# Pair 0's beginning: three small pieces of work put elsewhere in the queues

## What is computed

```python
def _dequant(qweight, scales, qzeros, g_idx):
    w = (qw[:, None, :] >> shifts[None, :, None] & 15).reshape(-1, N)
    z = ((qz[:, :, None] >> shifts[None, None, :] & 15) + 1).reshape(G, -1)
    return (w - z[g_idx]) * scales[g_idx]
...
Wg, Wu, Wd = _dequant(gate ...), _dequant(up ...), _dequant(down ...)
h = silu(xf @ Wg) * (xf @ Wu)
out = h @ Wd
...
x = x + 0.5 * ffn(layernorm(x))
x = x + attn(layernorm(x))
x = x + 0.5 * ffn(layernorm(x))
```

## Time and profile before

| | |
|---|---|
| three runs | 834.16, 834.57, 834.84 us |
| median | 834.57 us |
| the profiled execution: its time | 834.31 us |
| its span, first to last instruction | 832.5 us |
| TensorE busy | 816.9 us, 98% |
| TensorE idle in the first 30 us | 10.5 us |

### The profile page before, as it was taken

How to read it: one execution, slowest core, us unless ns; L and a number is a source line. 1 busy time by engine, 2 the same in 40 slices (tenths; PEclk the granted TensorE clock), 3 DMA queues, 4 the chain that set the end, 5 groups by cost and what they waited for, 6 DMA issues and landing times.

```text
span 832.5 us, 10583 instructions
## 1 busy us (share of the span) xinstructions
PE 816.9 (98%) x3944; PEld 671.9 (81%) x3944; DVE 493.2 (59%) x809; ACT 272.8 (33%) x471; POOL 251.2 (30%) x203
## 2 busy tenths in 40 slices
PE   5999999999999999999999999999999999999998
PEld 4777778878888888788888888888878888888786
DVE  7899945766554544547766785546346644443452
ACT  3333433455111111333656871121123311211221
POOL 5555614752115061303064371062411200110100
PEclk9999999999999999999999999999999999999999
DMA  5998968865754532334053159544444155444131
GB/s 157 268 347 276 311 202 286 335 254 222 277 189 140 170 133 70 105 107 152 1 178 126 39 178 373 207 139 166 126 154 154 43 197 170 133 150 153 29 102 51
DMA packets 73405, 143.04 MB, mean 172 GB/s; under 512 B 26092, under 2 KB 37028, under 8 KB 68362
## 3 DMA queue, kind: packets, MB, share of 16 engines
q1 hardware_dynamic: 66964, 131.10, 46.4%
q10 hardware_dynamic: 5526, 7.04, 2.4%
q0 software_dynamic: 864, 4.23, 1.8%
HBM read 104.30 MB, written 37.98 MB: 171 GB/s over the span
## 4 chain that ended last, share of the span: by engine, by line
PE 94%; DVE 2%; DMA 1%; POOL 1%; issue 1%; SPq 1%; ACT 1%; DVEq 0%; POOLq 0%
PE ps L811 52%; PE ps L804 38%; PE ps L822 2%; PE ps L1198 2%; DMA qs<-in_L_ffn_up_qweight 1%; DVE xn L1741 1%; SPq L561 1%; POOL wp L2213 0%; DMA zq_gu<-in_L_ffn_up_qzeros 0%; DVE stats L1718 0%; PE ps L890 0%; PE ps L1123 0%; POOL wd L2213 0%; DVE pT L1707 0%; ACT pr L1562 0%
## 5 line engine op out<-in xcount | busy, mean ns | idle before, releaser
L804 PE MATMUL ps<-blk,ring 128*128 128x512 f32 (+1 forms) x1386 | 321.2, 390 | 0.6 <-DVE u L1710 0.5
L804 PEld LDWEIGHTS ps<-blk,ring 128*128 128x128 f32 (+1 forms) x1386 | 256.5, 185 | 59.2 <-issue 1.2
L811 PE MATMUL ps<-wd,hT 128*128 128x512 f32 (+1 forms) x1056 | 251.7, 391 | 0.2
L811 PEld LDWEIGHTS ps<-wd,hT 128*128 128x128 f32 (+1 forms) x1056 | 196.9, 188 | 42.7 <-DVE h L1877 0.5
L2265 POOL TENSOR_TENSOR h<-h,u 128x512 f32<-128x512 f32 (+1 forms) x33 | 42.7, 1293 | 322.9 <-ACT h L1446 322.9
L811 PE MATMUL ps<-xT,wp 128*128 128x512 f32 x480 | 112.8, 391 | 0.2 <-POOL wp L2213 0.2
L811 PEld LDWEIGHTS ps<-xT,wp 128*128 128x128 f32 x480 | 89.8, 188 | 19.9 <-issue 0.6
L1710 DVE TENSOR_TENSOR u<-ps,p1s 128x512 f32<-128x512 f32 (+1 forms) x66 | 45.4, 687 | 97.0 <-PE ps L804 97.0
L1446 ACT ACTIVATE h<-h 128x512 f32<-128x512 f32 (+1 forms) x33 | 20.9, 632 | 177.7 <-DVE h L1710 177.7
L1710 DVE TENSOR_TENSOR h<-ps,p1s 128x512 f32<-128x512 f32 (+1 forms) x33 | 22.8, 691 | 64.3 <-PE ps L804 64.3
L1710 DVE TENSOR_TENSOR u<-ps,u 128x512 f32<-128x512 f32 (+1 forms) x66 | 45.6, 691 | 25.3 <-PE ps L804 24.3
(11 more groups left out here) (130 smaller groups left out, 887.2 us busy)
## 6 DMA issues: line engine op xcount, KB each, us to landing
ring<-wsaved SPq DMA_DIRECT2D x29, 1024.0 KB, 5.1
ring<-wsaved SPq DMA_DIRECT2D x33, 768.0 KB, 4.3
wsaved<-wp SPq DMA_DIRECT2D x10, 1024.0 KB, 5.2
stream<-xres SPq DMA_DIRECT2D x32, 256.0 KB, 2.3
xn<-stream SPq DMA_DIRECT2D x8, 1024.0 KB, 6.8
xres<-stream SPq DMA_DIRECT2D x32, 256.0 KB, 3.5
wfull<-wf ACTq DMA_DIRECT2D x20, 256.0 KB
wsaved<-wp SPq DMA_DIRECT2D x10, 512.0 KB, 4.9
```

Of the source, the lines that this page charges most:

```text
L804: mm = pe.matmul(ps[0:w, bank, :], ring[:, slot, which, a, kt, 0:w], blk[:, which, b, kt, :], start=not onto and kt == 0 and n == 0, stop= ...
L811: mm = pe.matmul(bank_ap, lhs(a), rhs(b), start=first and n == 0, stop=last and n == 2)
```

## The change

- DVE: the unpacking of down's zeros stands behind `tab_first` and the unpacking of unit 0, and no longer ahead of the one-hot steps. The step that makes `tab_first` is now number PACK + 3 of `s_tab`.
- SP: the loads of units 1 and 2 stand ahead of the transfers of down's indices and zeros. The transfer of down's scales to `rows_d` moves from SP to POOL's queue, near its start.
- POOL: the four index steps, and the wait for the table `rows_d`, stand behind the low half of unit 0.
- ACT: of the six transfers to `tab_rest` the first part's two stay where they were; the other four stand behind the high half of unit 2.
- PE: `keep_warm(5)` for `keep_warm(8)`, two tiles of x are turned ahead of `scales_zeros(0)`, and the `keep_warm(1)` there is gone.

```diff
-        ZERO_STEPS, ZERO_D_STEPS, TAB_STEPS = PACK + 2, 2 * PACK + 3, 2 * PACK + 4
+        ZERO_STEPS, TAB_STEPS, ZERO_D_STEPS = PACK + 2, PACK + 3, 2 * PACK + 4
...
-            return d_sz[i % 2], 16 * (i // 2 + 1)
+            return d_sz[i % 2], 16 * (i // 2 + 1 + (i + 1) % 2)
...
# SP
+            load_units(sp, [1])
 
             sp.wait_ge(s_cst, 4)
...
-            sp.dma_start(rows_d[:, 0:HID], scales[2]).then_inc(d_rows, 16)
-            load_units(sp, [1])
+            load_units(sp, [2])
             sp.wait_ge(s_tab, ZERO_D_STEPS)
             sp.dma_start(rows_d[:, HID:D_ROW].bitcast(BF16), zb_d).then_inc(d_rows, 16)
-            load_units(sp, [2])
             load_units(sp, [3, 4, 5])
...
# PE
-            keep_warm(8)
-
-            pe.wait_ge(s_oh, 3)
-            scales_zeros(0)
+            keep_warm(5)
             for r in range(RT):
                 if r == 2:
-                    keep_warm(1)
+                    pe.wait_ge(s_oh, 3)
+                    scales_zeros(0)
...
# ACT
+            def send_parts(n):
+
+                act.wait_ge(s_cut, PART_STEPS)
+                for m in range(2):
+                    row = FOLD * m + GK * n
+                    act.dma_start(tab_rest[row:row + GK, :], sc_part[n][SP_ROWS * m:SP_ROWS * (m + 1), :]).then_inc(d_cut_rest, 16)
+
...
                     w_hi(3 * i + 2)
+                    if i == 0:
+                        send_parts(1)
+                        send_parts(2)
...
             w_hi(1)
-
-            act.wait_ge(s_cut, PART_STEPS)
-            for m in range(2):
-                for n in range(3):
-                    row = FOLD * m + GK * n
-                    act.dma_start(tab_rest[row:row + GK, :], sc_part[n][SP_ROWS * m:SP_ROWS * (m + 1), :]).then_inc(d_cut_rest, 16)
+            send_parts(0)
             plain_top()
...
# DVE
             ln_var(0, (2, 3))
-            dve.wait_ge(d_zq_d, 16)
-            unpack_zeros(dve, tables, zq_d, zi_d, (zb_d, 1.0, 1.0))
             dve.wait_ge(d_idx_gu, 32)
...
             unpack(0)
+            dve.wait_ge(d_zq_d, 16)
+            unpack_zeros(dve, tables, zq_d, zi_d, (zb_d, 1.0, 1.0))
             dequantise(0)
...
# POOL
             cutter(lambda: pool.memset(zb_gu[Z_ROWS, :], Z_MARK))
+
+            pool.dma_start(rows_d[:, 0:HID], scales[2]).then_inc(d_sz[0], 16)
...
             scale_parts(pool, cutter)
-            pool.wait_ge(d_idx_d, 32)
-            indices(...)  (four steps)
             for u in range(UNITS):
...
                 w_lo(u)
                 m, i = unit(u)
+                if u == 0:
+                    pool.wait_ge(d_idx_d, 32)
+                    indices(...)  (the same four steps)
+                    pool.wait_ge(d_sz[0], 16)
+                    pool.wait_ge(d_rows, 16)
                 if u < 2:
-                    pool.wait_ge(d_rows, 32)
                     gather(u)
```

8 lines of the change are left out of this document (4 added, 4 removed).

## The result

The changed kernel takes 837.7 us (median of 10 runs, 835.47 to 838.88), the kernel before 834.71 us on the same chip (10 runs, 833.02 to 836.65). The ratio is 1.003, 95% interval 1.0021 to 1.004. Timed once more beside other kernels the change took 838.29 us (6 runs, 835.9 to 840.6), the kernel before 834.63; ratio 1.0049, interval 1.0034 to 1.0065. The change costs 3.0 to 3.7 us. The forecast was 836.6 us in a range of 835.0 to 838.8.

A forecast was written before the change was run, and what follows sets the result against it. TensorE was taken to run without holes behind 28 us, so delay before `scales_zeros(2)` counts fully: 29.9 - 27.76 - 0.15 = +2.0 us on 834.31 us, 836.3; with the median 0.26 us higher, 836.6 us, range 835.0 to 838.8.

The forecast's parts named there:

- Part 1, the zeros: DVE before `nmr`: removing down's zeros gains 0; behind unit 0's unpacking they cost 0.93 us, gate's tile 0 0.5 us late.
- Part 2, the clock: TensorE's new hole of some 2.7 us puts gate's tile 0 at the low clock, ending at 22.7 us; early turning worth 0.
- one of my own signs that the forecast is wrong: First products at full clock, `nmr` well before 10.7 us, or TensorE finding `tab_rest` there would show the forecast wrong.
- later still: Rival before `scales_zeros(2)`: parts need their old 6.65 us, or low clock covers gate's tile 0; 837.9 to 839.2 us; chance 0.11.
- Part 3, POOL: Index steps and gather before unit 1's low half: out at 22.15 us, up's tile 0 at 22.7, TensorE ready at 28.8.
- Part 4, the small transfers: Four transfers to `tab_rest` behind the first silu, issued 23.3 to 25.9 us, landing at 29.8: `scales_zeros(2)` at 29.9 us.
- lands with the second gather: Step before `scales_zeros(2)`: the last part lands with the second gather, forecast at 29.55 us, so parts at 29.8 us.
- The sum: At the end of the kernel: 29.9 - 27.76 - 0.15 = +2.0 us on 834.31 us; median forecast 836.6 us.
- The parts land in time: Rival at `scales_zeros(2)`: no wait for parts, TensorE goes on at 28.2 to 29.2 us; 834.9 to 835.9 us; chance 0.31.
- Not slower: Rival at `scales_zeros(2)`: TensorE's 1.05 us wait there swallows the delay; 834.1 to 834.6 us; no cost or under 0.5 gained 0.10.
- the rival by which DVE doesn't wait at `nmr`: Before `tab_first`: it comes 1.5 us earlier, first products up to 0.6 us earlier; more than 0.5 us won had 0.04.

The follow-up runs named there:

- parts early: The changed kernel with all six transfers to `tab_rest` issued at their old place, behind the high half of unit 1: 834.48 us, ratio 1.0000.
- store behind parts: The changed kernel with the last four transfers to `tab_rest` issued ahead of unit 2's store on ACT's queue instead of behind it: 835.58 us, ratio 1.0012.
- parts when ready on the change: The changed kernel with all six transfers issued as each is ready, ahead of unit 0's high half, and POOL's index steps before its first low half: 834.13 us.
- zeros ahead: The changed kernel with down's zeros unpacked ahead of the one-hot steps again, as before: 838.15 us, ratio 1.0046.
- loads back: The changed kernel with SP's loads of units 1 and 2 back at their old places: 836.28 us, ratio 1.0027.
- the change again: The changed kernel itself, unaltered, timed and profiled a second time against the kernel before: 838.29 us, ratio 1.0049.
- index steps first: The changed kernel with POOL's four index steps and their wait ahead of its first low half again: 835.75 us, ratio 1.0016.
- before + split: The kernel before with only four of the six transfers to `tab_rest` moved behind the copy and store of unit 2's high half: 834.76 us, ratio 1.0009.
- before with parts when ready: The kernel before with all six transfers to `tab_rest` issued as each is ready, ahead of unit 0's high half: 835.00 us, ratio 1.0005.
- first hole warmed: The changed kernel with 13 filling matmuls instead of 2 ahead of `scales_zeros(1)`: 835.92 us, ratio 1.0022.

## Why the prediction came out right, and where it was right for the wrong reason

**Part 1, the zeros: right.** `nmr` starts at 10.82 us as before and DVE waits 1.49 us for POOL; the removal is worth nothing. The eight instructions took 0.68 us in the new place, without a long one, where I had said 0.93 with the ninth: with `zb_d` it is 14.01 - 13.11 = 0.90. The Trainium skill, GPSIMD Engine Reference, section Key points, names contention between GpSimd and VectorE, in a 2-port mode or with two SBUF inputs. The trace agrees in part: the one instruction of 0.731 us in the earlier trace rows began at 9.08 us, beside POOL's L497 (9.04 to 9.78), and all eight are short where POOL is idle; but three others that began beside POOL's L496 took 0.16 to 0.21 us, and whether the page's conditions held no view shows. The first subtraction: 14.04 us, said 14.3. Gate's tile 0: 18.04, said 18.25.

**Part 2, the clock: the place was right, the time was not sure.** The low level in gate's tile 0 that I took as certain isn't in the profiled execution of the change: twelve matmuls in 3.01 us. First products at full clock were one of my own signs that the forecast is wrong: for this execution its road was wrong. The low level is on record in three others (parts early, store behind parts, and parts when ready on the change, all near 18.5 to 22.6 us), and the durations show it in three more whose record begins later (zeros ahead, 4.33 us for twelve; loads back and the change again, 8.45 us for 24). Where the parts leave early it is free, since POOL's low half for up's tile 0 takes as long (834.48 and 834.13 us). Where they stand behind the first silu, it makes them later, as my rival "later still" says. What the prediction didn't have at all is the second place: the wait for `tab_rest`. Behind it the clock falls in some executions, and there nothing covers it. Two profiles show it (4.33 us for 3.06, 1.3 us lost), and it stands in no term of my sum.

**Part 3, POOL: the order right, the match in part luck.** Unit 1's low half out at 21.20 + 1.28 = 22.48 us, said 22.15: the gather's issue stood 0.90 us behind the index steps, which my sum did not have, and the steps themselves were 0.2 us shorter. Up's tile 0 at 22.54, said 22.7, and TensorE ready at 25.79 + 2.98 = 28.77 us, said 28.8. But 22.7 and 28.8 were said for a low clock that did not come in this execution; for full clock I had 28.2. The 0.6 us that the low clock was to cost and the 0.6 us by which the road at full clock was longer than I had it cancel.

**Part 4, the small transfers: the number was near, the reason false.** `scales_zeros(2)` at 30.47 us, said 29.9; the second gather landed at 29.85, said 29.55, the parts at 30.33. By the profile alone the step "lands with the second gather" looks confirmed. It isn't: with the index steps first the gather came at 26.47 us and the parts at 30.19. In the ten profiles with the four parts late, the last part landed 3.7 to 6.6 us after its own issue, wherever the gather was. The Trainium skill, DMA: Bandwidth & Descriptors, section Queues, rings and completion order, says that an engine takes the queues in turn. Nothing here contradicts it, and no run here shows behind which transfers the parts waited; it was not the gather. What makes 3.7 us in one kernel and 6.6 in another I can't say. It isn't unit 2's store, nor the order of the two loads by itself.

**The sum: two errors that cancel.** It rested on "Behind 28 us TensorE runs without holes, so a microsecond won or lost before `scales_zeros(2)` at 27.76 us is one at the end", and gave back only the 0.15 us that TensorE waited for POOL at gate's tile 2. That is the step that failed. The list of TensorE's waits shows only what stops a matmul; the weight loads waited 1.9 us in all between 28 and 42 us, half a microsecond at a time, 1.5 us of it for POOL and DVE, and 1.1 us was real slack. On the profiled execution this gives +2.71 - 1.1 - 0.4 (small differences behind 450 us) = +1.2 us, measured +1.24, forecast +2.0. The median then lies 2.15 us above this execution, where my sum has 0.26. Filling both holes takes most of that away, so it goes mostly with the clock, for which the sum had nothing behind gate's tile 0. 836.6 us was said, 837.7 and 838.3 measured: that the number came so near is luck.

**The rivals.** "The parts land in time" did not happen in any run with the parts late. "Later still" is what the second profile of the change shows, by the second of its two causes: gate's tile 0 at the low clock and every issue later. I gave it 0.11, and ten of the sixteen executions of the change took 837.9 us or more, where that rival's range begins. "Not slower" is out. So is the rival by which DVE doesn't wait at `nmr`.

**A term that wasn't there.** The change moves the transfer of down's scales to `rows_d` from 8.7 us on SP's queue to 2.3 us on POOL's. I charged it nothing. The table of gate's and up's scales, `sc_gu`, is being loaded at that time, and POOL's L496 waits for it. In the three kernels with `rows_d` at 8.7 us whose profiles I have beside this (before, before + split, before with parts when ready) L496 starts at 8.00 to 8.03 us, without a wait for `sc_gu`. In the eleven profiles with `rows_d` at 2.3 us it starts at 7.92 to 8.75, in eight of them behind such a wait, 0.17 to 1.00 us long. `tab_first` moves with it: `scales_zeros(0)` starts at 12.98 to 13.01 us in the three, at 12.64 to 13.64 in the eleven. The two go together: in all fourteen profiles `scales_zeros(0)` starts 4.7 to 5.0 us behind L496. The two profiles of the change itself differ by it: no wait and 12.82 us in the first, 0.89 us and 13.47 in the second, so up to 0.65 us of the loss may lie here. No run moved `rows_d` by itself, so the cause is likely and not shown.

## What to carry to other kernels

A microsecond before a point is one at the end only if nothing behind it is near its limit: look at the waits of the weight loads too, and at how far the engine that prepares the weights is ahead, before pricing a delay (here 1.1 us was free). A small transfer issued while the 16 DMA engines were nearly full took 3.7 to 7.1 us here, and no sum of mine could say which, so it belongs early, into a stretch in which its engine idles. And where a change opens holes in TensorE's work, time the whole distribution: one profile may show the execution in which the clock stayed up.

## What the runs showed of the hardware

- The same hole lets the clock fall in some executions and not in others, and the place decides the price: nothing in gate's tile 0 when the parts have left before it (834.48 and 834.13 us), a later first silu and later parts when they stand behind it (24.19 against 21.09 us in the change's two profiles, 0.66 us of it a late start), and 1.3 us in up's tile 1. The heaps of runs are further apart, their means 2.3 to 2.7 us (before + split: 833.6 to 834.8 against 835.8 to 836.9 us; first hole warmed: 834.9 to 836.3 against 837.7 to 838.5). What else differs between them is in executions without a trace, and stays open.
- Filling matmuls on both holes brought the spread of the runs to 1.2 us (8 runs), from 3.4 us (10 runs) and 4.7 us (6 runs) of the change.
- The last part, 10.8 KB, took 3.7 to 6.6 us from its issue to landing between 23 and 32 us, at a DMA share near 0.9 to 1.0; issued between 11 and 15 us the six had all landed by 18.1 and 17.3 us, 3.5 and 2.2 us behind the last issue.
